# A four-layer convolution chain on one core: the input in three loads, constant products ahead of the first convolution, the result stored pair by pair

## The chip, the cores and the metric

The program runs on one core of a Trainium2 chip. The metric is device time in microseconds (us) of one execution; lower is better. Before the change three executions took 524.96, 528.49 and 530.88 us, so the median is 528.49 us. The engines are TensorE (PE for its matmuls, PEld for its weight loads), VectorE (DVE), ScalarE (ACT), GpSimd (POOL) and SyncE (SP), which only issues transfers. The program has no collective and nothing from another core.

## The reference, cut to what matters

`x` is a tensor of 16 images, 64 channels, 16 by 16 places, float32. Four layers are added to it one after the other, each on a group-normalized copy:

```python
def _gn(v, G=32, eps=1e-05):          # no gamma or beta
    ...
    return ((g - m) / jnp.sqrt(s + eps)).reshape(v.shape)

x = x + _L0_conv_ref(_gn(x), ...)     # 1x1 conv, group norm (8 groups), silu, a gated mixture of Gaussians, 1x1 conv, group norm, silu
x = x + _L1_conv_ref(_gn(x), ...)     # 3x3 depthwise conv and linear attention
x = x + _L2_conv_ref(_gn(x), ...)     # 8-head softmax attention over 256 places
x = x + _L3_conv_ref(_gn(x), ...)     # deformable 3x3 convolution
return x
```

The change touches the first steps of layer 0 and the way in which the result leaves the chip. The first steps of layer 0 are: statistics of `x` by image and pair of channels, `_gn(x)`, the 1x1 convolution with `pre_w`, and the group norm of its result, which has gamma and beta.

## The kernel before, in words

**Layout.** Two images make a pair: the 64 channels of the even image stand on partitions 0 to 63, those of the odd image on 64 to 127, and the 256 places along the free axis. So `x` is one tile of 128 x 8 x 256 floats (1 MB), with 8 pairs (`NP = 8`), and it stays on the chip from the first load to the last store. Each of the four layers is a block of the program in which every engine has its own straight list of instructions. Engines wait for each other by semaphores that count up; at the end of a block all engines meet.

**The head (`layer0`, L243 to L286).** SP (L261 to L267) issues the load of `avg2`, a constant 128 x 128 matrix, then `x` in two halves of four pairs, then all the weights of all four layers, one transfer each, in the order of the layers (`weights.load`, L204). DVE takes the statistics of the eight pairs in order (`bn_stats`, L274); ahead of pair 0 it waits for the first half of `x` and ahead of pair 4 for the second. Then comes `gn_x.vector` (L129): eight aggregations (L140), after which PE multiplies the means by `avg2` (L167), DVE forms the spread of the means (L146 to L148), PE multiplies the variances by `avg2` (L169), DVE adds eps (L150), ACT takes the square root (L174), and DVE makes `scale` (L152) and `shift` (L156, L159). DVE then writes `xn = x * scale + shift` pair by pair (L277). PE convolves two pairs at a time as soon as they are there (L366, four matmuls of 512 columns; a float32 matmul shows as two instructions in the profile). DVE takes the statistics of each convolved pair (L137) and `gn_1` runs in the same way, with `avg8` of the weights of layer 0.

**Steps that order this part.** PE's list is: wait for `avg2`; the two small matmuls of `gn_x`; wait for the weights of layer 0 (`weights.wait`, L209, which wants every one of the 11 transfers of that layer); the four matmuls of the convolution; the two of `gn_1`. POOL fills constant stacks for layer 2 with `memset` (L464, L468), and between the third and the fourth it waits until all eight `xn` are there (L250). ACT has nothing to do in the head but the two square roots. `signals.own` is a counter by which DVE waits for its own last instruction (`Steps`, L83); its count after `gn_x` is `signals.own_steps`.

**`keep_clock` (L177)** is a helper that issues `count` products of `avg2` with itself into a part of PSUM that nobody reads. It is used already at the end of layer 0 (20 of them, 40 instructions in the profile) and in layer 1.

**The rest of layer 0** is a loop over the pairs in which ACT makes squares and exponentials (L415, L418), DVE polynomials and products (L337, L342), and PE sums them up (L382).

**The tail (`layer3`, L1109 to L1568).** Layer 3 goes over the pairs 0 to 7 in order, in nine steps (taps) each. In each step PE spreads weights over rows and columns (L1500, L1510), ACT copies the column part (L1404), DVE multiplies (L1335) and PE sums over the taps (L1523). When a pair is done, DVE adds the sum and the bias to `x[:, n]` (L1339) and raises `added`; `added` starts at 2 (L1322), so it is `n + 3` once pair `n` is final. Nothing reads or writes `x[:, n]` after that in this layer. SP loads the interpolation weights (`hats`, L1236) of two pairs at a time; its last piece of work is `next_chunk(3)`, which issues four transfers for pair 6 and four for pair 7, the latter once enough products of pair 5 have been made. After the block of layer 3 there is a last block (L1593 to L1597), in which SP stores all of `x` in one transfer of 1 MB and waits for it.

Of the kernel before, what the change touches and what calls it, by code (L numbers as in the profile page):

```python
# [24 lines left out]
NP = B // 2  # L25
# [190 lines left out]
def layer0(nc, ins, signals, weights, x, avg2, stacks):  # L216
    with Memory(nc, "L0") as m:
# [14 lines left out]
        s1, s2 = y2[0:32, 4, 0:NP], y2[:, 6, 0:NP]  # L232
        par_ps = y2[:, 4, 0:NP * NPAR].rearrange("p (n k) -> p n k", n=NP)

        avg_in, *x_in = m.sems("avg_in x_in0 x_in1")
        (xn_ready, y1_ready, norm1_ready, z_ready, s1_ready, h1_ready, s2_ready, h2_ready, h2_w_ready,
         par_ready, exp_in, exp_out, coef_ready) = m.sems(
            "xn_ready y1_ready norm1_ready z_ready s1_ready h1_ready s2_ready h2_ready h2_w_ready "
            "par_ready exp_in exp_out coef_ready")
        (uu_ready, e_ready, poly_ready, t_ready, t_used, norm2_ready, out_ready, added, odd_added) = m.sems(  # L240
            "uu_ready e_ready poly_ready t_ready t_used norm2_ready out_ready added odd_added")
# [1 line left out]
        with nc.Block() as block:  # L243
            @block.gpsimd
            def _(pool):

                stacks.fill_q(pool, 0)
                stacks.fill_k(pool, 0)
                stacks.fill_q(pool, 1)
                pool.wait_ge(xn_ready, NP)  # L250
                stacks.fill_k(pool, 1)
                stacks.fill_q(pool, 2)
                pool.wait_ge(norm1_ready, 1)
                stacks.fill_k(pool, 2)
                stacks.fill_q(pool, 3)
                stacks.fill_k(pool, 3)
                for p in range(1, NP, 2):
                    pool.wait_ge(out_ready, p + 1)
                    pool.tensor_tensor(x[:, p, :], x[:, p, :], xn[:, p, :], ALU.add).then_inc(odd_added, 1)

            @block.sync  # L261
            def _(sp):
                sp.dma_start(avg2[:], ins["avg2"]).then_inc(avg_in, 16)
                for h in range(2):
                    half = slice(4 * h, 4 * h + 4)
                    sp.dma_start(x[:, half], ins["x"].rearrange("(n e) c h w -> (e c) n (h w)", e=2)[:, half]).then_inc(x_in[h], 16)
                weights.load(sp, range(4))  # L267

            @block.vector
            def _(dve):  # L270
                for p in range(NP):
                    if p % 4 == 0:
                        dve.wait_ge(x_in[p // 4], 16)
                    dve.bn_stats(signals.x_bn[:, p, :], x[:, p, :]).then_inc(signals.x_stats, 1)  # L274
                gn_x.vector(dve)
                for p in range(NP):
                    dve.tensor_scalar(xn[:, p, :], x[:, p, :], gn_x.scale[:, p:p + 1], gn_x.shift[:, p:p + 1],  # L277
                                      ALU.mult, ALU.add).then_inc(xn_ready, 1)

# [78 lines left out]

            @block.tensor
            def _(pe):  # L360
                pe.wait_ge(avg_in, 16)
                gn_x.tensor(pe)
                weights.wait(pe, 0)
                for h in range(NP // 2):
                    pe.wait_ge(xn_ready, 2 * h + 2)
                    pe.matmul(y1[:, 2 * h:2 * h + 2, :], w_pre[:], xn[:, 2 * h:2 * h + 2, :], start=True, stop=True).then_inc(y1_ready, 1)  # L366
                gn_1.tensor(pe)
                pe.wait_ge(z_ready, NP)
                pe.matmul(s1, w_s1[:], pooled[:], start=True, stop=True).then_inc(s1_ready, 1)
                pe.wait_ge(h1_ready, 1)  # L370
                pe.matmul(s2, w_s2[0:32, :], h1[:], start=True, stop=True).then_inc(s2_ready, 1)
                pe.wait_ge(h2_w_ready, 1)
                pe.matmul(par_ps, same_group[:], h2_w[:], start=True, stop=True).then_inc(par_ready, 1)
                pe.sem_inc(t_used, 2)
                pe.wait_ge(coef_ready, 1)
                with pe.Fori(0, NP // 2) as i:
                    for q in range(2):
                        k = 2 * i + q
                        pe.matmul(y2[:, ds(k, 1), :], w_post[:], z[:, ds(k, 1), :], start=True, stop=False)
                        pe.wait_ge(t_ready, k + 3)  # L380
                        for j in range(NB):
                            mm = pe.matmul(y2[:, ds(k, 1), :], w_post[:], t[:, q, j:j + 1, :], start=False, stop=(j == NB - 1))  # L382
                        mm.then_inc(t_used, 1)
                gn_2.tensor(pe)
                keep_clock(pe, avg2, y1[:, 6], 20)

            @block.scalar
            def _(act):
                gn_x.scalar(act)
                gn_1.scalar(act)  # L390
                act.wait_ge(norm1_ready, 1)
                for p in range(NP):
# [716 lines left out]
                        context(c, 0, k - 6)  # L1109


def layer3(nc, ins, signals, weights, x, avg2):

# [8 lines left out]
    with Memory(nc, "L3") as m:  # L1124
# [97 lines left out]
        with nc.Block() as block:  # L1222
            @block.sync
            def _(sp):
# [43 lines left out]
                sp.wait_ge(later_stored, 256)  # L1268
                for c in range(1, B // CH):
                    next_chunk(c)  # L1270

            @block.gpsimd
            def _(pool):
# [303 lines left out]
def program(nc, ins, out, layers=4):  # L1577
    Memory.semaphores = ExitStack()
    with Memory.semaphores, Memory(nc, "all") as m:
# [9 lines left out]
            if layers > 2:  # L1589
                layer2(nc, ins, signals, weights, x, avg2, stacks)  # L1590
        if layers > 3:
            layer3(nc, ins, signals, weights, x, avg2)
        with nc.Block() as block:  # L1593
            @block.sync
            def _(sp):
                sp.dma_start(out.rearrange("(n e) c h w -> (e c) n (h w)", e=2), x[:]).then_inc(x_out, 16)
                sp.wait_ge(x_out, 16)  # L1597

# [98 lines left out]
```

## Time and profile before

| | |
|---|---|
| three executions | 524.96, 528.49, 530.88 us; median 528.49 us |
| span of the profiled execution | 528.0 us, first to last instruction |
| what lies around the span | not shown apart; the median of the executions is 0.49 us above this span |
| PE, DVE, ACT, POOL busy | 439.1, 342.4, 288.9, 132.8 us |
| layer 0, layer 1, layer 2, layer 3 begin at | 0, 88, 193 and 348 us of the span |

The span runs from the first instruction to the last on any engine. A busy share is an average over stages of different kinds: PE has 83%, but in the first thirteenth of the execution it waits for most of the time. All times in the rows below are microseconds from the start of the span unless they are marked ns. PEclk is the clock that TensorE was granted, as a share of 2.4 GHz.

### The profile page before, as it was taken

To read this page: it belongs to the slowest core of one execution; us is meant where nothing else is said; L and a number is where in the kernel's file an instruction comes from. 1 tells how busy PE (TensorE), PEld (TensorE's weight loads), DVE (VectorE), ACT (ScalarE), POOL (GpSimd) and SP (SyncE) were. 2 spreads that over 40 slices of the span, in tenths; PEclk is the share of its full clock that TensorE was granted. 3 is DMA by queue.
4 is the path that set the end of the run, shared out by engine and by line. 5 is a ranking of instruction groups with operands and counts; after the bars stand their busy time and mean duration, and the time that the engine had idled before them with its cause. 6 is when DMAs were issued, how large, how long until landed. Compare 5 with 4: busy or idle time off the path is not lost. (4 is left out here: it accounts for less than half of the span.)

```text
span 528.0 us, 9368 instructions
## 1 busy us (share of the span) xinstructions
PE 439.1 (83%) x3406; PEld 231.3 (44%) x3406; DVE 342.4 (65%) x668; ACT 288.9 (55%) x511; POOL 132.8 (25%) x162
## 2 busy tenths in 40 slices
PE   0527768899999887679999999939898999999995
PEld 0216648555455664223333333324443454454442
DVE  4549876233344568978999996251654778777784
ACT  1279955131532437047878778722865578486441
POOL 4420004000000005744422212031364428065000
PEclk9956997999999988559999999957977999999999
DMA  5500000900000004952200000016390480933302
GB/s 142 164 0 1 0 0 1 197 1 1 0 1 0 1 0 107 279 175 67 73 27 3 3 2 4 0 47 160 100 226 15 89 181 2 217 55 68 67 2 79
DMA packets 20767, 33.79 MB, mean 64 GB/s; under 512 B 5657, under 2 KB 15497, under 8 KB 19957
## 3 DMA queue, kind: packets, MB, share of 16 engines
q1 hardware_dynamic: 16724, 23.70, 18.9%
q0 software_dynamic: 2176, 6.35, 4.3%
q10 hardware_dynamic: 1824, 3.19, 2.3%
q8 instruction: 26, 0.43, 0.4%
q14 instruction: 17, 0.13, 0.1%
HBM read 16.21 MB, written 4.64 MB: 39 GB/s over the span
## 5 line engine op out<-in xcount | busy, mean ns | idle before, releaser
L1335 DVE TENSOR_TENSOR L_s<-L_row_ps,L_cols 128x1024 f32<-128x1024 f32 x72 | 87.6, 1218 | 9.3 <-PE L_row_ps L1500 7.5
L910 DVE TENSOR_REDUCE L_mx<-L_ring 128x2 f32<-128x512 f32 x128 | 83.3, 686 | 12.4 <-PE L_ring L1034 11.8
L965 ACT ACTIVATE L_e<-L_ring 128x512 f32<-128x512 f32 x128 | 73.7, 597 | 21.4 <-PE L_ring L1047 19.3
L1523 PE MATMUL L_acc<-L_s,L_t_sb 128*64 128x256 f32 x576 | 81.6, 406 | 1.1 <-DVE L_s L1335 1.0
L1404 ACT ACTIVATE L_cols<-L_col_ps 128x512 f32<-128x512 f32 x72 | 42.8, 596 | 48.9 <-PE L_col_ps L1510 48.5
L1034 PE MATMUL L_ring<-stacks_k_st,stacks_q_st 64*128 64x256 bf16 x256 | 51.0, 301 | 7.0 <-DMA stacks_k_st<-L_k_parts 4.7
L1523 PEld LDWEIGHTS L_acc<-L_s,L_t_sb 128*64 128x64 f32 x576 | 36.0, 140 | 35.9 <-DVE L_s L1335 19.8
L1047 PE MATMUL L_ring<-stacks_q_st,stacks_k_st 64*128 64x256 bf16 x256 | 47.2, 282 | 1.2 <-DMA stacks_q_st<-L_m_parts 1.2
L1500 PE MATMUL L_row_ps<-L_hats,L_sel 48*128 48x512 bf16 x144 | 44.6, 392 | 0.0
L1067 PE MATMUL L_ctx_ps<-L_e,L_v_x 128*32 128x256 f32 x512 | 41.5, 398 | 0.0
L1311 DVE COPY L_t_sb<-L_acc 128x192 f32<-128x192 f32 x48 | 17.1, 357 | 31.4 <-PE L_acc L1491 31.4
L1034 PEld LDWEIGHTS L_ring<-stacks_k_st,stacks_q_st 64*128 64x128 bf16 x256 | 15.9, 98 | 43.8 <-DVE L_mx L910 24.2
L382 PE MATMUL L_y<-L_t,all_w_post 128*128 128x256 f32 x96 | 25.3, 418 | 11.5 <-DVE L_t L342 11.5
L1510 PE MATMUL L_col_ps<-L_hats,L_sel 48*128 48x512 bf16 x72 | 28.7, 400 | 7.0 <-DMA L_hats<-L_parts 5.0
L1491 PE MATMUL L_acc<-all_w_all,L_xn 64*128 64x192 f32 x96 | 26.8, 362 | 5.0 <-DVE L_t_sb L1311 2.7
L382 PEld LDWEIGHTS L_y<-L_t,all_w_post 128*128 128x128 f32 x96 | 19.4, 208 | 17.1 <-DVE L_t L342 14.2
L1491 PE MATMUL L_col_ps<-all_w_all,L_xn 64*128 64x192 f32 x96 | 26.7, 360 | 0.0
L853 POOL MEMSET L_v_x<- 128x1024 f32 x1 | 1.0, 951 | 101.7 <-POOLq L496 101.7
L1200 POOL TENSOR_TENSOR L_hat<-L_hat,L_mask 64x768 f32<-64x768 f32 x9 | 16.3, 1812 | 40.1 <-ACT L_hat L1382 40.1
L415 ACT ACTIVATE L_uu<-L_z,L_minus_mu,L_inv 128x256 f32 x48 | 24.4, 586 | 1.3 <-DVEq L314 1.3
L633 ACT ACTIVATE L_sq<-L_t_ps 128x1024 f32<-128x1024 f32 x4 | 4.1, 1024 | 34.9 <-PE L_t_ps L716 34.9
L656 PE MATMUL L_xs_ps<-L_stack,L_w_tap 128*128 128x512 f32 x48 | 22.7, 601 | 0.0
(270 smaller groups left out, 814.2 us busy)
## 6 DMA issues: line engine op xcount, KB each, us to landing
L_hats<-L_parts SPq DMA_DIRECT2D x28, 216.0 KB, 5.0
L_hat<-L_offsets SPq DMA_DIRECT2D x20, 192.0 KB, 4.7
L_mask<-L_offsets SPq DMA_DIRECT2D x10, 192.0 KB, 4.9
stacks_q_st<-L_q_parts SPq DMA_DIRECT2D x12, 128.0 KB, 3.9
stacks_k_st<-L_k_parts ACTq DMA_DIRECT2D x12, 128.0 KB, 4.8
stacks_q_st<-L_q_parts POOLq DMA_DIRECT2D x12, 128.0 KB, 2.7
stacks_k_st<-L_k_parts POOLq DMA_DIRECT2D x12, 128.0 KB, 2.9
L_stack<-L_xpad SPq DMA_DIRECT2D x7, 162.0 KB, 5.8
```

Of the source, the lines that this page charges most:

```text
L382: mm = pe.matmul(y2[:, ds(k, 1), :], w_post[:], t[:, q, j:j + 1, :], start=False, stop=(j == NB - 1))
L910: dve.tensor_reduce(mx[:, n % 2, :, head], ring[:, place(step) % 3].rearrange("p (q s) -> p q s", q=2), AX.X, ALU.max).then_inc(max_read, 1)
L965: act.activation(e[:, k], ring[:, 3 + v % 3], ACT.Exp, scale=HD2 ** -0.5).then_inc(e_ready, 1)
L1034: mm = pe.matmul(ring[:, place(step) % 3, q * N:(q + 1) * N], rows_of(q_st, n, h, p)[:, q * P:(q + 1) * P], rows_of(k_st, n, h, p), start= ...
L1047: mm = pe.matmul(ring[:, 3 + v % 3, t * N:(t + 1) * N], rows_of(k_st, c, h, p)[:, t * P:(t + 1) * P], rows_of(q_st, c, h, p), start=True, ...
L1067: mm = pe.matmul(ctx_ps[32 * j:32 * j + 32, g * N:(g + 1) * N], v_x[:, c % 2, t, 4 * g + j, :], e[:, 4 * g + j, t * N:(t + 1) * N], start= ...
L1335: dve.tensor_tensor(s[:, q], row_ps[:, q], cols[:, t % 3:t % 3 + 1].broadcast_to([P, 2, 2 * N]), ALU.mult).then_inc(s_ready, 1)
L1404: act.activation(cols[:, v % 3], col_ps[:, c % 2], ACT.Copy).then_inc(col_read, 1)
L1491: mm = pe.matmul(out, xn[rows, b, k // 3 * P:(k // 3 + 1) * P], w_all[rows, k % 3 * TW:(k % 3 + 1) * TW], start=True, stop=True)
L1500: mm = pe.matmul(row_ps[:, v % 2, h], sel[0:3 * H, h], hats[0:3 * H, n % 2, :, t * N:(t + 1) * N], start=True, stop=True)
L1510: pe.matmul(col_ps[:, c % 2], sel[C:C + 3 * H, 2], hats[C:C + 3 * H, n % 2, :, t * N:(t + 1) * N], start=True, stop=True).then_inc(col_rea ...
L1523: mm = pe.matmul(acc[C * e:C * e + C, b, 0:N], t_sb[:, b, h, (KK * e + t) * C:(KK * e + t + 1) * C], s[:, q, h, e * N:(e + 1) * N], start= ...
```

## The change

The change has four parts, and one that follows from the second.

1. `x` is loaded in three lots: pairs 0 and 1, pairs 2 and 3, pairs 4 to 7. The load of `avg2` is issued between the first lot and the second. The first lot and `avg2` raise one semaphore (`x_in[0]`), the second and the third lot raise the other (`x_in[1]`). DVE waits for the first two transfers ahead of pair 0 and for both others ahead of pair 2.
2. PE waits for the first lot and `avg2`, issues 20 constant products, then the matmuls of `gn_x`, and after the wait for the weights 8 more constant products ahead of the convolution.
3. ACT writes `xn` for pairs 2, 3, 6 and 7, after waiting for `scale` and `shift`; DVE writes pairs 0, 1, 4 and 5. PE's waits ahead of its four matmuls and POOL's wait ahead of its fourth fill follow that.
4. The last block's store of 1 MB is gone. In layer 3 SP stores each pair (128 KB) when `added` says that it is final, after its last `next_chunk`; the last block only waits for all eight.

```diff
@@ layer0
-        avg_in, *x_in = m.sems("avg_in x_in0 x_in1")
-        (xn_ready, y1_ready, norm1_ready, ...
+        x_in = m.sems("x_in0 x_in1")
+        (xn_ready, xn_by_scalar, y1_ready, norm1_ready, ...
@@ gpsimd
-                pool.wait_ge(xn_ready, NP)
+                pool.wait_ge(xn_ready, 4)
@@ sync
-                sp.dma_start(avg2[:], ins["avg2"]).then_inc(avg_in, 16)
-                for h in range(2):
-                    half = slice(4 * h, 4 * h + 4)
-                    sp.dma_start(x[:, half], ins["x"].rearrange("(n e) c h w -> (e c) n (h w)", e=2)[:, half]).then_inc(x_in[h], 16)
+                for h, lot in enumerate((slice(0, 2), slice(2, 4), slice(4, NP))):
+                    sp.dma_start(x[:, lot], ins["x"].rearrange("(n e) c h w -> (e c) n (h w)", e=2)[:, lot]).then_inc(x_in[min(h, 1)], 16)
+                    if h == 0:
+                        sp.dma_start(avg2[:], ins["avg2"]).then_inc(x_in[h], 16)
                 weights.load(sp, range(4))
@@ vector
                 for p in range(NP):
-                    if p % 4 == 0:
-                        dve.wait_ge(x_in[p // 4], 16)
+                    if p in (0, 2):
+                        dve.wait_ge(x_in[p // 2], 32)
                     dve.bn_stats(signals.x_bn[:, p, :], x[:, p, :]).then_inc(signals.x_stats, 1)
                 gn_x.vector(dve)
-                for p in range(NP):
+                gn_x.scaled = signals.own_steps
+                for p in (0, 1, 4, 5):
                     dve.tensor_scalar(xn[:, p, :], x[:, p, :], gn_x.scale[:, p:p + 1], gn_x.shift[:, p:p + 1],
                                       ALU.mult, ALU.add).then_inc(xn_ready, 1)
@@ tensor
-                pe.wait_ge(avg_in, 16)
+                pe.wait_ge(x_in[0], 32)
+                keep_clock(pe, avg2, y2[:, 6], 20)
                 gn_x.tensor(pe)
                 weights.wait(pe, 0)
+                keep_clock(pe, avg2, y2[:, 6], 8)
                 for h in range(NP // 2):
-                    pe.wait_ge(xn_ready, 2 * h + 2)
+                    pe.wait_ge((xn_ready, xn_by_scalar)[h % 2], 2 * (h // 2) + 2)
                     pe.matmul(y1[:, 2 * h:2 * h + 2, :], w_pre[:], xn[:, 2 * h:2 * h + 2, :], start=True, stop=True).then_inc(y1_ready, 1)
@@ scalar
                 gn_x.scalar(act)
+                act.wait_ge(signals.own, gn_x.scaled)
+                for p in (2, 3, 6, 7):
+                    act.activation(xn[:, p, :], x[:, p, :], ACT.Identity, scale=gn_x.scale[:, p:p + 1],
+                                   bias=gn_x.shift[:, p:p + 1]).then_inc(xn_by_scalar, 1)
                 gn_1.scalar(act)
@@ layer3, sync
                 for c in range(1, B // CH):
                     next_chunk(c)
+                for n in range(NP):
+                    sp.wait_ge(added, n + 3)
+                    sp.dma_start(out.rearrange("(n e) c h w -> (e c) n (h w)", e=2)[:, n], x[:, n]).then_inc(x_out, 16)
@@ program, last block
-                sp.dma_start(out.rearrange("(n e) c h w -> (e c) n (h w)", e=2), x[:]).then_inc(x_out, 16)
-                sp.wait_ge(x_out, 16)
+                sp.wait_ge(x_out, 16 * NP)
```

## Rows read from the trace of the kernel before

**Rows 1.** The page: PE's clock in 40 slices of 13.2 us, in tenths.

```profile
PEclk9956997999999988559999999957977999999999
```

**Rows 2.** Timeline of the head: start, length, engine, line, operation, count, [idle before, releaser].

```profile
0.74 0.40 SPq L263 DMA_DIRECT2D all_avg<-in_avg  x1
1.20 0.96 SPq L266 DMA_DIRECT2D all_x<-in_x  x2
...
5.58 2.90 DVE L274 BATCH_NORM_STATS2 all_x_bn<-all_x 128x6 f32<-128x256 f32 x8 [5.58 <-DMA all_x<-in_x]
...
9.37 0.57 PE L167 MATMUL L_y<-L_gn_x_mv,all_avg 128*128 128x8 f32 x2 [9.37 <-DVEq L144]
...
10.59 0.60 PE L169 MATMUL L_y<-L_gn_x_var,all_avg 128*128 128x8 f32 x2 [0.66 <-DVE L_gn_x_var L148]
...
12.30 2.67 DVE L277 TENSOR_SCALAR L_xn<-all_x,L_gn_x_scale,L_gn_x_shift 128x256 f32<-128x256 f32 x8
13.18 5.88 PE L366 MATMUL L_y<-L_xn,all_w_pre 128*128 128x512 f32 x8 [2.00 <-DVE L_xn L277]
```

**Rows 3.** Instructions of tile x, then of tile avg, issued before 3 us: transfers' time to landing.

```profile
DMA to landing us min/median/max: 4.4/4.9/5.4
...
DMA to landing us min/median/max: 1.9/2.9/3.9
```

**Rows 4.** Timeline of the convolution's passes (weight loads) and the statistics behind them.

```profile
15.02 0.33 PEld L366 LDWEIGHTS L_y<-L_xn,all_w_pre 128*128 128x128 f32 x1 [0.52 <-issue]
15.88 0.33 PEld L366 LDWEIGHTS L_y<-L_xn,all_w_pre 128*128 128x128 f32 x1 [0.52 <-issue]
...
17.58 0.22 PEld L366 LDWEIGHTS L_y<-L_xn,all_w_pre 128*128 128x128 f32 x1 [0.52 <-issue]
18.04 0.19 PEld L366 LDWEIGHTS L_y<-L_xn,all_w_pre 128*128 128x128 f32 x1 [0.24 <-issue]
18.24 1.62 DVE L137 BATCH_NORM_STATS2 L_gn_bn<-L_y 128x6 f32<-128x256 f32 x4 [0.51 <-PE L_y L366]
...
20.92 0.39 PE L167 MATMUL L_y<-L_gn_mv,all_avg 128*128 128x8 f32 x2 [1.85 <-DVEq L144]
```

**Rows 5.** Stretches: length, busy time (instructions) of each engine, PEclk, DMA share, GB/s.

```profile
13.00:17.60 4.60, 4.42 (x6) 1.85 (x7) 3.36 (x11) 0.00 (x0) 2.57 (x2) 1.00 0.57 152
24.00:35.00 11.00, 1.90 (x6) 1.18 (x6) 2.28 (x10) 8.53 (x26) 5.29 (x3) 0.52 0.04 13
80.00:82.00 2.00, 2.00 (x10) 2.00 (x11) 1.16 (x6) 1.83 (x3) 0.00 (x0) 0.50 0.00 0
86.00:87.00 1.00, 1.00 (x11) 1.00 (x10) 0.96 (x4) 0.00 (x0) 0.38 (x1) 1.00 0.00 0
```

**Rows 6.** Timeline of PE: the 20 constant products at the end of layer 0.

```profile
79.75 7.64 PE L182 MATMUL L_y<-all_avg 128*128 128x128 f32 x40
```

**Rows 7.** Lines: ACT's pairwise normalization in layer 3; timeline of ACT at layer 2's start.

```profile
L1413 ACT ACTIVATE L_xn<-all_x,L_gn_shift,L_gn_scale x6: 588/590/591, 408.7 to 492.0; 128x256 f32<-128x256 f32 x6
...
195.16 0.21 ACT L174 ACTIVATE L_gn_sd<-L_gn_sp 128x8 f32<-128x8 f32 x1 [1.17 <-DVE L_gn_sp L150]
198.89 0.69 ACT L953 ACTIVATE L_e<-L_ring,all_l_vec 128x512 f32<-128x512 f32 x1 [3.52 <-PE L_ring L1003]
```

**Rows 8.** Timeline of the tail: SP's last transfers, the last add and the store.

```profile
482.16 11.55 SPq L1236 DMA_DIRECT2D L_hats<-L_parts  x8
...
522.36 0.48 DVE L1339 SCALAR_TENSOR_TENSOR all_x<-L_acc,all_l_vec,all_x 128x256 f32<-128x256 f32 x1 [1.19 <-PE L_acc L1523]
523.12 0.43 SPq L1596 DMA_DIRECT2D out_x<-all_x  x1
```

**Rows 9.** Transfers: the store's landing, a stretch of it, and a 128 KB load.

```profile
out_x<-all_x SPq DMA_DIRECT2D x1, 1024.0 KB, 4.5
...
525.00:526.00 1.00, 0.00 (x0) 0.00 (x0) 0.00 (x0) 0.00 (x0) 0.00 (x0) 1.00 1.03 347
...
all_grid<-in_grid SPq DMA_DIRECT2D x1, 128.0 KB, 2.8
```

More of the change, by code:

```diff
@@ L233, in layer0 @@
         par_ps = y2[:, 4, 0:NP * NPAR].rearrange("p (n k) -> p n k", n=NP)
-        avg_in, *x_in = m.sems("avg_in x_in0 x_in1")
-        (xn_ready, y1_ready, norm1_ready, z_ready, s1_ready, h1_ready, s2_ready, h2_ready, h2_w_ready,
+        x_in = m.sems("x_in0 x_in1")
+        (xn_ready, xn_by_scalar, y1_ready, norm1_ready, z_ready, s1_ready, h1_ready, s2_ready, h2_ready, h2_w_ready,
          par_ready, exp_in, exp_out, coef_ready) = m.sems(
-            "xn_ready y1_ready norm1_ready z_ready s1_ready h1_ready s2_ready h2_ready h2_w_ready "
+            "xn_ready xn_by_scalar y1_ready norm1_ready z_ready s1_ready h1_ready s2_ready h2_ready h2_w_ready "
             "par_ready exp_in exp_out coef_ready")
@@ L1109, in _, with layer3 @@
                         context(c, 0, k - 6)
-def layer3(nc, ins, signals, weights, x, avg2):
+def layer3(nc, ins, signals, weights, x, avg2, out, x_out):
     KK = 9
@@ L1591, in program @@
         if layers > 3:
-            layer3(nc, ins, signals, weights, x, avg2)
+            layer3(nc, ins, signals, weights, x, avg2, out, x_out)
         with nc.Block() as block:
```

## The prediction

> **What bounds the kernel now.** I read four views: the page for the whole, the timeline of the first 20 us, the stretches of TensorE's clock, and the timeline of the last 10 us. The change touches only the two ends of the execution, some 20 us at the start and 6 us at the end, so the question is what ends last at each end, and whether a shift of the start is passed on.
>
> The head is one chain. DVE has nothing until 5.58 us, when the first half of `x` lands [rows 2]. Then the eight statistics run without a gap for 2.90 us, so the second half is not waited for; it was issued about 0.47 us after the first and took 5.4 us, landing at 7.1 us [rows 3]. That is just when DVE comes to pair 4. Aggregation, the two small matmuls at 9.37 and 10.59 us and the small steps between them follow, `xn` begins at 12.30, the convolution at 13.18 and ends at 19.06. PE does nothing before 9.37 us but wait.
>
> The convolution is bound by PE's clock. Its passes (two for each float32 matmul) come 0.86 us apart (15.02, 15.88), the last ones 0.46 us apart (17.58, 18.04) [rows 4]. 512 columns in 0.86 us is the 1.2 GHz level, in 0.46 us near the 2.4 GHz one. The clock column reads 1.00 for the same stretch [rows 5], so in the head I go by the spacing of the passes and not by that column. DVE waits 0.51 us before its last four statistics, which end at 19.86 us; everything behind hangs on that. The clock is low again from 24 to 35 us [rows 5], since PE idles between the few small matmuls there, so what is gained in the head is the time of the convolution and nothing of the later stages.
>
> Over the whole, the page's clock line shows other low stretches, in slices 3 and 4, 17 and 18, and 27 to 31 [rows 1]. Where their borders fall can move when the start is shifted. That is noise for this prediction: three executions of the same kernel spread over 5.9 us.
>
> **The change, part by part.** *Three loads.* The third lot raises the same semaphore as the second, and DVE wants both ahead of pair 2. So pairs 2 and 3 wait for the whole of `x`. The bytes ahead of that moment are the same 1 MB plus 64 KB, the last lot is issued at 2.13 instead of 1.67 us (one more issue of 0.46 us, half of the 0.96 us of two) and the first bytes are asked for at the same 0.74 us, so I keep the landing of all of `x` at 7.1 us, with 6.7 and 7.6 as ends. Pairs 0 and 1 are done before. Six statistics remain at 2.90/8 = 0.36 us each: 7.1 + 2.2 = 9.3 us against 8.48 before. The loads alone cost +0.85 us (0.4 to 1.3). The mean matmul could then start at 9.37 + 0.85 = 10.2 us. The weights are issued 0.46 us later; the convolution waited for `xn` and not for them [rows 2], and it will not start sooner by more than a few tenths in any case below, so that is hidden.
>
> *Twenty constant products.* They stand ahead of the mean matmul on PE's queue, so DVE, and behind it ACT and PE itself, wait for them. They start when the first lot and `avg2` have landed. `avg2` is issued at 1.20 us; the two constants of 64 KB issued in the first 3 us took 1.9 us (alone) and 3.9 us (beside `x`) [rows 3], so it lands between 3.1 and 5.1 us; I take 4.1. The first lot, issued at 0.74, needs no more than the 4.4 us that a lot of twice its size took, so 5.1 at the latest. The 20 products are 40 passes. The same 20 took 7.64 us at the end of layer 0 [rows 6], with ten passes in 2.0 us at the low level (0.21 us each) and eleven in 1 us at the high one [rows 5], where the passes are half as long (0.107 us). All low they would take 8.5 us. In the convolution the low level lasted some 4.4 us from its start (13.18 to 17.6): then 20.6 passes are slow and 19.4 fast, 4.4 + 2.1 = 6.5 us. Between the two cases I take 7.1 us. The products then end at 4.1 + 7.1 = 11.2 us, and the mean matmul starts at 11.2 instead of 9.37: +1.85 us, which contains the 0.85 of the loads.
>
> *At the high level* the two small matmuls are shorter: 0.39 us [rows 4] instead of 0.57 and 0.60 [rows 2], together −0.38 us. *The eight products* are 16 fast passes, 1.7 us. From the variance matmul to the convolution there were 2.59 us; less 0.2 for the faster matmul that is 2.4, and the products fit in it behind the matmul's own time (0.39 + 1.7 = 2.1). I cost them at nothing; all low they are 3.4 us and stick out by some 1.6.
>
> The convolution starts at 13.18 + 1.85 − 0.38 = 14.65 us. Its eight passes at 0.43 us (half of 0.86) put the last start at +3.0, its end at +3.6, and the last two statistics (1.62/4 = 0.4 each) at +4.4 us: 19.05 us instead of 19.86. **The head gives −0.8 us**: −2.25 from the convolution, −0.38 from the small matmuls, +1.85 from the wait behind the products. It would be −1.8 if the products were done in time (loads +0.85 alone), −2.25 with the loads at +0.4.
>
> *ACT's four pairs.* An Identity of one pair takes 0.59 us [rows 7]. ACT is idle there; it delivers pairs 2 and 3 some 1.2 us after `shift`, while PE wants them 0.9 (first two pairs by DVE) + 0.85 us after it. Hidden. DVE comes free 1.3 us sooner, for the first statistics behind the convolution, which at the high clock would otherwise wait about 0.6 us; the sum above contains that. A table load is a possible price, since Identity follows a square root: at 195.16 a square root and at 198.89 an Identity run with no load between them [rows 7], so none. POOL's fourth fill starts when DVE's four are done, about as now; nobody waits for it before layer 2.
>
> *The store.* The last add ends at 522.84, the store is issued at 523.12 (the blocks' meeting lies between) and lands 4.5 us later [rows 8, 9], at 527.6; the span ends 0.4 us after. At 347 GB/s the 1 MB takes 3.0 us of those 4.5; an eighth takes 0.4. So the last pair's store lands 1.9 us after its issue, as the 64 KB load did [rows 3]. Issued at 523.0: 524.9, end 525.3. **The tail gives −2.7 us**; a load of 128 KB beside others took 2.8 us [rows 9], with which it would be −1.8. The other seven stores: SP is done with its hats at 493.71 [rows 8]; by then the adds of pairs 0 to 4 are long done and that of pair 5 about now (the last pair's is at 522.4, two pairs later), so some six stores go out in about 3 us, behind the hats of pair 7, which that pair wants when pair 6 is nearly through. Pair 6 leaves during pair 7. SP has nothing else queued. So they are hidden; without that cover they would be 6 x 0.4 us of transfer.
> The Trainium skill (DMA: Bandwidth & Descriptors, Rules for kernel authors) speaks against this part: it wants many small transfers made one, with 1 MiB or more for full bandwidth. Its fit in the section Anatomy of one DMA, measured on transfers issued by GpSimd, about 2.0 us + bytes/436e3, gives 4.4 us for the old store, and the trace's 4.5 agrees; for the last pair it gives 2.3, by which the tail would be −2.3. The rule does not bite as long as the seven others stay off the path.
>
> **Sum.** 528.0 − 0.8 − 2.7 = 524.5 us of span. The median of the runs shown is 0.49 above that execution's span, so 525.0 us, −3.5 us or 0.66%.
>
> **The rivals.** *Clock up early.* If the clock rises about 4.4 us or less after the first product and `avg2` lands near 3.1 us, the products end by 9.6 us, ahead of the statistics. Then head −1.8 to −2.25, total 523.5 to 524.0. For it: the lower case of the row. Against it: 20 passes too many have to fit, and both conditions must hold.
>
> *The warm-up costs more than it gives*, the slow side. Its place is PE's queue ahead of the mean matmul. With 8.5 us of slow passes from 4.1 the matmul starts at 12.6 (+3.25), nothing is saved on the small ones, the eight products take 3.4 us: variance matmul at 13.85, convolution at 13.85 + 0.6 + 3.4 = 17.85, and slow as before 6.7 us to 24.5 against 19.86: head +4.7, total 528.5 + 4.7 − 2.7 = 530.5 us. It decides as soon as the head loses more than the 2.7 of the tail: a fast convolution that starts after 18.1 us, or a slow one after 15.9. Against it: both times that PE was kept busy, the clock rose within 4.4 and some 6.2 us (13.18 to 17.6, 79.75 to 86) [rows 4, 5].
>
> *The shift is not passed on.* The ends give what I say, but low-clock stretches of the later layers grow or shrink with the shift. The layers' start-ups are chains of short steps on PE, so a border can cost or give 2 us either way; with the spread of the runs 522 to 528.5.
>
> *The change does not do what it says* in one point already: three loads do not let DVE go on with pair 2 earlier. That is in the sum.
>
> **How the numbers follow.** Forecast (524 to 526.5) 0.50; early clock 0.20; products too long 0.08; shifted borders 0.22. A difference of over 1% (5.3 us) is about what a measurement of this kernel can tell from no change. The forecast alone lies 1.8 us short of it: I give 0.08 of its 0.50 to faster, 0.09 of the early clock's, 0.07 of the last, 0.24 in all. Slower needs 533.8 us, which even the slow rival reaches only with a high draw: 0.03. The rest, 0.73, is within 1%. The range: 523.5 less a low draw of 1.7 is 521.8; above, the forecast with the tail at −1.8 and products of 8.5 us is 527.3, and the shifted borders take it to 528.3.
>
> **What would show it.** DVE's statistics end near 9.3 us with a gap of about 2 us behind pair 1 (right), or run on (wrong). PE's first product starts near 4.1 us; the mean matmul starts right behind the last one, later than 10.2. The convolution's passes are 0.43 us apart and its eight take 3.6 us. No table load stands between ACT's square root and its four Identities. The last store lands 1.9 us after its issue, and the span ends some 2.5 us after the last add instead of 5.2. I am wrong if the statistics are not the six behind one wait, if the clock falls again ahead of the convolution, or if the time between 20 us and the last add changes by more than 2 us.

## The result, and the profile after

The changed kernel takes 521.12 us (median of four runs, 520.05 to 522.25) against 527.53 us of the kernel before: ratio 0.988, 95% interval 0.9835 to 0.9925. Six more runs gave 521.48 against 526.94 us, ratio 0.9891 (0.9863 to 0.9919). It is faster by 5.5 to 6.4 us; I had forecast 3.5 us, the right way but too little, and the first median lies 0.7 us under my range. One run of the experiments, 531.19 us, fell into a slower state of the chip and is left out below.

The profiled execution has a span of 519.2 us and took 520.96 us, so 1.8 us lie around a span. That puts the profiled execution of before (span 528.0) at about 529.8 us, a long draw, and not near the median as I had read it.

The head of the changed kernel; columns as in [rows 2]:

```profile
0.74 0.45 SPq L264 DMA_DIRECT2D all_x<-in_x  x1
1.25 0.45 SPq L266 DMA_DIRECT2D all_avg<-in_avg  x1
...
3.81 0.75 DVE L274 BATCH_NORM_STATS2 all_x_bn<-all_x 128x6 f32<-128x256 f32 x2 [3.81 <-DMA all_avg<-in_avg]
...
3.83 6.67 PE L182 MATMUL L_y<-all_avg 128*128 128x128 f32 x40 [3.83 <-DMA all_avg<-in_avg]
...
7.37 2.06 DVE L274 BATCH_NORM_STATS2 all_x_bn<-all_x 128x6 f32<-128x256 f32 x6 [2.81 <-DMA all_x<-in_x]
...
9.46 0.64 DVE L140 BATCH_NORM_AGGREGATE L_gn_x_mv<-all_x_bn 128x2 f32<-128x6 f32 x8
...
10.34 0.29 PE L167 MATMUL L_y<-L_gn_x_mv,all_avg 128*128 128x8 f32 x2
...
11.52 2.03 PE L182 MATMUL L_y<-all_avg 128*128 128x128 f32 x16
...
12.79 2.08 ACT L395 ACTIVATE L_xn<-all_x,L_gn_x_shift,L_gn_x_scale 128x256 f32<-128x256 f32 x4 [0.67 <-DVE L_gn_x_shift L159]
...
13.57 3.70 PE L369 MATMUL L_y<-L_xn,all_w_pre 128*128 128x512 f32 x8
...
18.11 0.64 DVE L140 BATCH_NORM_AGGREGATE L_gn_mv<-L_gn_bn 128x2 f32<-128x6 f32 x8
```

Three things are to be seen. DVE does two statistics and then waits 2.81 us: the second and third load share a semaphore, so pair 2 waits for all of `x`. The products end at 10.50 us, 0.4 us behind DVE's aggregations (10.10); but the mean matmul starts 0.24 us behind the aggregations, as it did before the change (0.21), so in this profile it does not wait for the products. And the convolution takes 3.70 us instead of 5.88 [rows 2], with its passes 0.43 us apart where [rows 4] had 0.86 and 0.46. `gn_1` begins its aggregations at 18.11; in the profile before that was 19.90.

The tail, in the timeline of the changed kernel and in its list of transfers (KB, us to landing):

```profile
516.55 0.48 DVE L1349 SCALAR_TENSOR_TENSOR all_x<-L_acc,all_l_vec,all_x 128x256 f32<-128x256 f32 x1 [1.19 <-PE L_acc L1533]
517.06 0.33 SPq L1280 DMA_DIRECT2D out_x<-all_x  x1
```

```profile
out_x<-all_x SPq DMA_DIRECT2D x1, 128.0 KB, 1.7
```

From the start of the last add to the end of the span it is 2.65 us, against 5.64 before (528.0 − 522.36 [rows 8]): 3.0 us less.

So between these two profiles the ends account for 1.8 + 3.0 = 4.8 us. The head's part varies: over the four profiles with the old head and the five with the changed one in the table below, its means are 19.5 and 18.4 us, which is 1.2 us, and 4.2 for both ends. The two profiles differ by 8.8 us; the other 4 us lie in layers 2 and 3. This table follows milestones through all profiles (us; the last column is the span, the others are the stretches between them). "Old" ends are those of the kernel before, "new" those of the changed one.

| kernel | head, to gn_1's aggregations | to layer 1 | layer 1 | layer 2 | layer 3 to add of pair 0 | pair 0 to last add | last add to end | span |
|---|---|---|---|---|---|---|---|---|
| before | 19.90 | 68.1 | 104.7 | 155.3 | 62.2 | 112.2 | 5.64 | 528.0 |
| before, second profile | 19.74 | 68.1 | 105.2 | 154.8 | 61.1 | 112.1 | 5.63 | 526.6 |
| changed | 18.11 | 67.9 | 105.5 | 153.7 | 59.5 | 111.9 | 2.65 | 519.2 |
| changed, second profile | 18.13 | 67.9 | 105.1 | 154.0 | 60.1 | 111.9 | 2.63 | 519.8 |
| new tail alone | 19.70 | 68.3 | 105.7 | 153.6 | 61.3 | 112.2 | 2.58 | 523.3 |
| new head alone | 18.48 | 67.9 | 105.5 | 153.9 | 59.6 | 112.0 | 5.68 | 523.0 |
| changed, no products | 21.80 | 68.1 | 105.1 | 154.9 | 60.1 | 112.2 | 2.60 | 524.7 |
| own semaphore for each lot | 18.86 | 68.1 | 105.2 | 154.4 | 59.6 | 112.0 | 2.61 | 520.7 |
| early products | 17.21 | 67.9 | 105.4 | 155.0 | 61.1 | 112.0 | 2.61 | 521.2 |
| VectorE alone | 18.37 | 68.1 | 105.1 | 154.5 | 60.7 | 112.1 | 2.59 | 521.4 |
| twelve products | 17.91 | 67.9 | 104.7 | 153.7 | 59.8 | 114.6 | 2.65 | 521.2 |
| changed, products in layer 3 | 18.44 | 68.2 | 104.9 | 154.3 | 56.7 | 111.9 | 2.59 | 517.0 |
| the same, second profile | 18.59 | 68.1 | 105.0 | 152.3 | 57.8 | 112.0 | 2.62 | 516.4 |
| both mended | 18.97 | 67.9 | 104.9 | 155.2 | 57.0 | 111.9 | 2.56 | 518.5 |
| old ends, products in layer 3 | 18.83 | 68.1 | 105.2 | 153.0 | 60.0 | 114.4 | 5.61 | 525.1 |

The column "to layer 1" moves by 0.4 us in all: what the head gains is passed on whole through the rest of layer 0. For the three kernels with two profiles each, layer 2 differs by 0.3 to 2.0 us between the two and layer 3's start-up by 0.6 to 1.1 us; the difference of 2.7 us in that start-up between the first profiles of before and changed is larger than that.

### The profile page after: what moved, and what is told of

Its sections match the earlier page's. It is cut to its first block and busy times, and to the rows that moved or that the text cites. A ratio compares the mean times of both kernels' runs of the same rounds, so it can differ in the third digit from the quotient of the medians.

```text
span 519.2 us, 9486 instructions
## 1 busy us (share of the span) xinstructions
PE 439.2 (85%) x3462; PEld 235.8 (45%) x3462; DVE 341.0 (66%) x664; ACT 291.8 (56%) x515; POOL 133.0 (26%) x162
## 5 line engine op out<-in xcount | busy, mean ns | idle before, releaser
L1533 PE MATMUL L_acc<-L_s,L_t_sb 128*64 128x256 f32 x576 | 79.5, 398 | 1.4 <-DVE L_s L1345 1.2
L1501 PEld LDWEIGHTS L_acc<-all_w_all,L_xn 64*128 64x128 f32 x96 | 18.5, 203 | 9.2 <-DVE L_t_sb L1321 4.3
```

Of the source, the lines that this page charges most:

```text
L1501: mm = pe.matmul(out, xn[rows, b, k // 3 * P:(k // 3 + 1) * P], w_all[rows, k % 3 * TW:(k % 3 + 1) * TW], start=True, stop=True)
L1533: mm = pe.matmul(acc[C * e:C * e + C, b, 0:N], t_sb[:, b, h, (KK * e + t) * C:(KK * e + t + 1) * C], s[:, q, h, e * N:(e + 1) * N], start= ...
```

## The experiments

**The two ends alone.** Theory A: the ends explain the gain, the rest is chance. Theory B: the new head makes later layers faster. Theory C: the pairwise stores help layer 3.

```diff
 # new tail alone: the kernel before, with
+                for n in range(NP):
+                    sp.wait_ge(added, n + 3)
+                    sp.dma_start(out...[:, n], x[:, n]).then_inc(x_out, 16)
 # new head alone: the changed kernel, with the last block's
+                sp.dma_start(out..., x[:]).then_inc(x_out, 16)
```

> The kernel before with nothing but the pairwise store. Theory A (the two ends explain the gain, the rest of the profiled pair's difference is where TensorE's low-clock stretches happened to fall in layer 3): the span ends 2.65 us after the last add instead of 5.64, so 3.0 us less than before, ratio 0.994. Theory B (the head's new timing moves the low-clock stretches of the later layers, every time): also 3.0 us less here, since the head is the old one. Theory C (the stores or the missing 1 MB transfer help layer 3 itself): more than 4.5 us less, and pairs 6 and 7 of layer 3 take less time.

> The changed kernel with the old store of 1 MB in the last block: the changed head alone. Theory A: 1.8 us less than before, ratio 0.9966. Theory B: 3.4 to 5.8 us less, and layer 3 again starts its pair 0 sooner after its own start than before. Theory C: 1.8 us less at most.

The tail alone: 524.53 against 527.43 us, ratio 0.9938 (0.9905 to 0.997), 3.3 us. The head alone: 525.46, ratio 0.9957 (0.9934 to 0.9981), 2.3 us. Both hold what the traces give (3.0 and 1.2 to 1.8); their sum is 5.6 us. Theory C falls: pair 0 to the last add is 112.2 us with the new tail and with the old one. B had wanted 3.4 to 5.8 us of the head alone and stands at the edge of the head's interval of 1.0 to 3.5 us; a smaller effect of the head is not excluded.

**Without the constant products.**

```diff
-                keep_clock(pe, avg2, y2[:, 6], 20)
...
-                keep_clock(pe, avg2, y2[:, 6], 8)
```

> The changed kernel without the 20 and the 8 constant products. Theory A: the passes of the first convolution are 0.86 us apart again for most of it, and the small matmuls take 0.57 us: the head is 0.4 to 0.9 us longer than in the kernel before (statistics 1.0 us later, ScalarE's share little), total 3.0 - 0.6 = 2.4 us less than before, ratio 0.9955. Theory B: as A if it is the clock in the head that carries over, so the same number here.

525.26 us, ratio 0.9961 (0.9934 to 0.9989): 3.7 us more than the changed kernel's 0.9891. The timeline of this kernel's head:

```profile
7.52 2.06 DVE L274 BATCH_NORM_STATS2 all_x_bn<-all_x 128x6 f32<-128x256 f32 x6 [3.05 <-DMA all_x<-in_x]
...
10.46 0.56 PE L167 MATMUL L_y<-L_gn_x_mv,all_avg 128*128 128x8 f32 x2 [10.46 <-DVEq L144]
...
14.28 6.68 PE L367 MATMUL L_y<-L_xn,all_w_pre 128*128 128x512 f32 x8 [2.00 <-DVE L_xn L278]
```

The mean matmul starts at 10.46 us although no product stands ahead of it, and at 10.34 with them. So the loads, not the products, set that time in these two profiles. It is close: in three other profiles with the same head the products took 7.07 to 7.13 us and the mean matmul came at 10.66 to 10.81, some 0.3 to 0.5 us later than the aggregations would have let it. The products give 3.7 us here: 3.0 of the convolution (6.68 to 3.70), 0.4 of the small matmuls. Without them the three loads and ScalarE's share make the head 1.9 us *longer* than before (21.80 against 19.90); I had expected 0.4 to 0.9.

**A semaphore for each lot.**

```diff
+        x_in = m.sems("x_in0 x_in1 x_in2")
...
-                    if p in (0, 2):
-                        dve.wait_ge(x_in[p // 2], 32)
+                    if p in (0, 2, 4):
+                        dve.wait_ge(x_in[p // 2], 16 if p else 32)
```

> The changed kernel with a semaphore of its own for the third load, so that the statistics of pairs 2 and 3 wait for the second lot only. The gap of 2.8 us behind pair 1 shrinks and the statistics end 0.5 to 0.7 us sooner. If the 20 products set the time of the mean matmul (they end at 10.5, the statistics and aggregations at 10.1), the total moves by less than 0.2 us against the changed kernel; if the statistics set it, it falls by 0.6.

520.25 us, ratio 0.9865 (0.9828 to 0.9902), not told apart from the changed kernel. Its head:

```profile
3.69 7.55 PE L182 MATMUL L_y<-all_avg 128*128 128x128 f32 x40 [3.69 <-DMA all_avg<-in_avg]
5.54 0.75 DVE L274 BATCH_NORM_STATS2 all_x_bn<-all_x 128x6 f32<-128x256 f32 x2 [1.11 <-DMA all_x<-in_x]
7.10 1.41 DVE L274 BATCH_NORM_STATS2 all_x_bn<-all_x 128x6 f32<-128x256 f32 x4 [0.81 <-DMA all_x<-in_x]
8.54 0.64 DVE L140 BATCH_NORM_AGGREGATE L_gn_x_mv<-all_x_bn 128x2 f32<-128x6 f32 x8
...
11.08 0.29 PE L167 MATMUL L_y<-L_gn_x_mv,all_avg 128*128 128x8 f32 x2
```

Here the order is clear: the aggregations end at 9.2 us and the mean matmul waits for the products until 11.08. The same 20 products took between 6.16 and 7.55 us in seven profiles, as the clock rose sooner or later. No gain from the earlier statistics is shown, as expected where the products are the bound.

**Early products, and fewer of them.**

```diff
 # early: a semaphore for each load as above; GpSimd fills a tile first, PE works on it before anything has landed
+                pool.memset(warm[:], 1.0).then_inc(coef_ready, 1)
...
+                pe.wait_ge(coef_ready, 1)
+                keep_clock(pe, warm, y2[:, 6], 22)
                 pe.wait_ge(x_in[0], 32)
-                keep_clock(pe, avg2, y2[:, 6], 20)
 # fewer: own semaphores, and
-                keep_clock(pe, avg2, y2[:, 6], 20)
+                keep_clock(pe, avg2, y2[:, 6], 12)
```

> A mended head: a semaphore for each load, and the constant products made of a tile that GpSimd fills first (22 of them), so that they start at about 1.3 us instead of 3.8 and end before the statistics do. The statistics and aggregations end at 9.2 as in the kernel with its own lot, whose mean matmul still waited for the products until 11.1. If the products ahead of the mean matmul are the step that I sized wrongly and the one that still costs, the mean matmul starts at 9.3 to 9.6, gn_1's aggregations at 17.1 to 17.4, and the total falls by 0.8 to 1.6 us against the changed kernel (ratio to before 0.985). If they are hidden by something else, nothing.

> The kernel with a semaphore for each lot, and 12 constant products instead of 20 ahead of the mean matmul. With 20 the mean matmul waited for them until 11.08 us while the aggregations ended at 9.2. All low, 24 passes take 5.1 us: from 3.7 they end at 8.8, so the mean matmul starts at 9.4. If the clock has risen by the time of the convolution, its passes are 0.43 us apart and gn_1's aggregations start at 17.3 us; total 0.8 us under the changed kernel. If 12 are too few to raise it, some passes are 0.86 us apart and the aggregations start at 18 to 19.5 us: no gain or a loss of 1 us.

```profile
0.99 7.71 PE L182 MATMUL L_y<-L_warm 128*128 128x128 f32 x44 [0.99 <-POOL L_warm L247]
...
9.36 0.36 PE L167 MATMUL L_y<-L_gn_x_mv,all_avg 128*128 128x8 f32 x2 [0.66 <-DVEq L144]
...
17.21 0.64 DVE L140 BATCH_NORM_AGGREGATE L_gn_mv<-L_gn_bn 128x2 f32<-128x6 f32 x8
```

These are rows of the early products: the mean matmul starts at 9.36 as before the change, and gn_1 0.9 us sooner than in the changed kernel, as expected. In time it is 520.97 us, ratio 0.9869 (0.9839 to 0.9899) against 0.9891 on the same chip: the right way, not resolved. Twelve products took 5.49 us and were enough to raise the clock (the mean matmul took 0.39 us, the convolution 3.70). But that matmul came at 10.03 and `gn_1` at 17.91, not at 9.4 and 17.3, because all of `x` had landed only at 7.83. Timed they gave 522.01 us and 0.9907 (0.9878 to 0.9937): the expected 0.8 us is not shown.

**ScalarE's share.**

```diff
-                for p in (0, 1, 4, 5):
+                for p in range(NP):
...   # and ACT's four pairs go; the waits of PE and POOL as before the change
```

> The changed kernel with VectorE normalizing all eight pairs again. With the convolution's passes 0.43 us apart, VectorE begins its statistics of the convolved pairs 1.3 us later, of which 0.6 us is not covered: gn_1's aggregations start at 18.7 instead of 18.1 us. The rival: ScalarE's share is hidden and gives nothing, 18.1 as now.

522.2 us, ratio 0.989 (0.9862 to 0.9919) against 0.9891: no difference. By the profile the head is 18.37 instead of 18.11 (18.7 was expected), but DVE goes on behind the mean matmul 0.22 us later as well (10.88 against 10.66), since the last lot landed at 7.61; what is left for the share is 0.04 us. The rival holds: VectorE starts the statistics 0.8 us later, but runs them without a gap, at 0.34 us each.

**Where the rest lies.** The kernel before and the changed one again:

> The kernel before, unchanged, for a second profile. Measured in the first profile: 62.2 us from layer 3's start (ScalarE's table load) to the add of its pair 0, against 59.5 to 59.6 us in the three profiles of kernels with the constant products in the head, and 61.3 and 60.1 in two without. Theory A (the place of the low-clock stretches in layer 3 is a draw of the execution): this time differs from 62.2 and may lie anywhere from 59.5 to 62. Theory B (the head decides it): again 61.5 to 62.5.

> The changed kernel again, for a ratio over more runs and a second profile. The two ends give 4.8 us by the traces, the two halves timed alone 3.3 and 2.3 us, together 5.6. Theory A: ratio 0.989 to 0.991, since the 6.4 us of four runs held a share of chance. Theory B (the parts together do more than each): 0.987 or less.

Layer 3's start-up took 61.1 us where the first profile of before had 62.2, and 60.1 where the changed kernel had 59.5. So it varies by some 1 us from one execution to the next. 61.1 is in A's range and 0.4 us under B's, but it is still above both times of the changed kernel. The changed kernel's ratio of 0.9891 is within A's 0.989 to 0.991. The draws do not mix well: 61.1 to 62.2 in the three profiles with the old head (without products in layer 3), 59.5 to 61.1 in the eight with the new one.

The traces show where the difference arises. Some 34 us into layer 3 PE waits for the first hats. The kernel before, then the changed one (timeline of PE, then stretches as in [rows 5]):

```profile
384.92 1.97 PE L1523 MATMUL L_acc<-L_s,L_t_sb 128*64 128x256 f32 x8 [0.71 <-DVE L_s L1335]
```

```profile
381.00:387.00 6.00, 3.75 (x17) 1.38 (x18) 3.31 (x3) 3.68 (x7) 4.55 (x8) 0.66 0.69 192
387.00:389.00 2.00, 2.00 (x9) 0.77 (x8) 1.11 (x1) 1.07 (x2) 0.12 (x1) 0.50 1.05 268
399.00:405.00 6.00, 4.84 (x22) 2.48 (x24) 1.49 (x2) 4.17 (x8) 3.44 (x2) 0.58 0.01 3
```

```profile
379.53 0.37 PE L1520 MATMUL L_col_ps<-L_hats,L_sel 48*128 48x512 bf16 x1 [1.70 <-DMA L_hats<-L_parts]
381.91 1.08 PE L1533 MATMUL L_acc<-L_s,L_t_sb 128*64 128x256 f32 x8 [0.93 <-DVE L_s L1345]
```

```profile
378.00:384.00 6.00, 3.52 (x24) 1.42 (x26) 3.75 (x4) 4.25 (x8) 4.47 (x8) 1.00 0.79 205
390.00:396.00 6.00, 4.85 (x22) 2.67 (x24) 1.55 (x3) 2.19 (x5) 0.73 (x2) 0.52 0.49 87
```

Before, the clock is low behind this wait (the same eight matmuls take 1.97 us instead of 1.08) and again at 399; in the changed kernel only once, at 390. In all three old-head profiles the wait is 1.94 to 2.08 us and the clock falls behind it. With a new head the wait is 1.70 to 1.86 us; in five of the eight profiles (both of the changed kernel, the new head alone, own semaphores, twelve products) the clock stays up there and the start-up takes 59.5 to 60.1 us, in the other three it falls and the start-up takes 60.1 to 61.1. So the difference is, in the main, one low stretch more or less. Why the hats come later with the old head no run shows, and the wait does not decide alone: of three profiles with 1.70 us the clock fell in one.

In layer 3 PE stands still at the start (348 to 350 us), and its clock is low until the offset convolution has run for some microseconds. Products there test what this costs:

```diff
                 weights.wait(pe, 3)
+                keep_clock(pe, avg2, row_ps[:, 0, 0], 5)
...
                     weigh(0, k, k, k)
+                    if k == 0:
+                        keep_clock(pe, avg2, row_ps[:, 0, 0], 4)
...
+                keep_clock(pe, avg2, row_ps[:, 0, 0], 8)
                 pe.wait_ge(hats_in[0], 64)
```

> The changed kernel with 17 more constant products in layer 3: 5 behind its group norm, 4 behind its first weighing matmuls, 8 ahead of the wait for the first hats. It tests whether low-clock stretches in layer 3's start-up carry the part of the time that neither end explains. From layer 3's start to the add of pair 0 it was 59.5 to 62.2 us in ten profiles. If the stretches matter (theory A), the stretch at the start ends sooner, the four weighings (0.68 us) and the first offset convolution (4.15 us against 2.8) get shorter, and that time falls to 57 to 58.5 us, the total by 1.5 to 2.5 us against the changed kernel. The rival: the chain there is bound by DMA (offsets and hats), the time stays at 59.5 to 61 and the total is unchanged.

> The head with early products and a semaphore for each lot, and the 17 products in layer 3. If both gains hold and add, 0.9 us (head) and 1.5 to 2.5 us (layer 3) under the changed kernel: about 518.5 us, ratio to before 0.983 to 0.985. By the rival of the run before, only the head's 0.9: 520.5.

The changed kernel, then the one with the products (the timeline of PE, then the stretch from 354 to 356 us, columns as in [rows 5]):

```profile
352.89 0.68 PE L1501 MATMUL L_acc<-all_w_all,L_xn 64*128 64x192 f32 x1 [1.84 <-DVE L_t_sb L1321]
...
356.74 4.15 PE L1473 MATMUL L_row_ps<-L_stack,all_w_off 128*32 128x256 f32 x48
```

```profile
354.00:356.00 2.00, 1.21 (x6) 0.71 (x8) 0.65 (x2) 0.63 (x2) 2.00 (x4) 0.50 0.94 199
```

```profile
351.66 1.99 PE L182 MATMUL L_row_ps<-all_avg 128*128 128x128 f32 x8
353.58 0.43 PE L1502 MATMUL L_acc<-all_w_all,L_xn 64*128 64x192 f32 x1
...
356.19 2.80 PE L1474 MATMUL L_row_ps<-L_stack,all_w_off 128*32 128x256 f32 x48
```

```profile
354.00:356.00 2.00, 1.11 (x12) 0.60 (x8) 0.71 (x2) 0.66 (x2) 2.00 (x4) 1.00 1.09 217
```

The clock rises before the weighings instead of during the convolution, which takes 2.80 us instead of 4.15; layer 3's start to the add of pair 0 falls to 56.7 us, in a second profile to 57.8. Timed: 518.9 us, ratio 0.9846 (0.9805 to 0.9887); again, later, 519.63 and 0.9872 (0.984 to 0.9904). With the mended head as well: 520.12 and 0.9847 (0.9806 to 0.9888), where I had expected 518.5 us. So in the profiles the low-clock stretches of this start-up cost 1.7 to 3.4 us; all 17 products came in one edit, and what each place gives is not separated. These kernels have the lowest medians measured, 1.4 to 2.6 us under the changed one, in ratios whose intervals overlap its own.

The mended head did not add its 0.9 us. In that profile the 22 early products were over sooner and `x` came later, and its rows show what follows:

```profile
0.99 6.68 PE L182 MATMUL L_y<-L_warm 128*128 128x128 f32 x44 [0.99 <-POOL L_warm L247]
9.78 0.36 PE L167 MATMUL L_y<-L_gn_x_mv,all_avg 128*128 128x8 f32 x2 [2.11 <-DVEq L144]
11.09 3.12 PE L182 MATMUL L_y<-all_avg 128*128 128x128 f32 x13
```

PE stood still for 2.11 us ahead of the mean matmul (0.66 in the first profile with early products), and the passes of the eight products, of which the last line shows 13, were 0.24 us apart; the granted clock was 0.50 from 12 to 14 us. They took 3.6 us in place of 2.03 and held the convolution up until 14.54; `gn_1` began at 18.97 instead of 17.21.

**Chance or the head?** The same products with the old ends:

> The kernel before with the 17 constant products in layer 3 and nothing else: old head, old store. With the changed ends and these products it was 518.9 us. By the traces the two ends are worth 1.8 + 3.0 = 4.8 us. Theory A (the ends give 4.8 us and the rest of the difference between the two kernels, 1.0 to 1.6 us, is where low-clock stretches of layer 3's start-up fall by chance): 518.9 + 4.8 = 523.7 us, ratio to before 0.994, and layer 3's start to the add of pair 0 takes 56.5 to 57 us as in the two kernels that have the products. Theory B (the changed head makes the later layers faster by 1 us or more): 524.7 us or more, ratio 0.996 or more.

> The changed kernel with the 17 products in layer 3 once more, on the same chip as the one with the old ends. Theory A: 4.3 to 5.3 us under it. Theory B: 6 us or more under it.

525.32 us (520.92 to 528.41, ratio 0.9949, 0.9917 to 0.9982) against 519.63. The difference is 5.7 us by the medians and 0.0077 or 4.1 us by the ratios: A had wanted 4.3 to 5.3, B 6 or more. Layer 3's start-up took 60.0 us; A's 56.5 to 57 did not come, and that is 2.2 to 3.3 us more than in the three profiles with the new head and the same products. It holds two later waits, 1.93 us for hats and 1.95 for ScalarE, where those three have one of 2.75 to 3.02 for hats. The profile shows another reason why the times do not decide:

```profile
414.00:419.00 5.00, 3.55 (x26) 1.89 (x28) 2.44 (x5) 1.55 (x4) 0.00 (x0) 0.98 0.99 229
419.00:422.50 3.50, 3.50 (x17) 1.14 (x13) 2.26 (x2) 1.17 (x3) 0.00 (x0) 0.54 1.03 241
422.50:427.00 4.50, 4.50 (x35) 2.11 (x35) 3.06 (x5) 3.33 (x6) 0.72 (x1) 1.00 1.07 215
```

Here the clock was low for some 3.5 us in the middle of layer 3, right after a wait of 1.45 us for hats at 416 to 418, and the pairs 1 to 7 took 114.4 us instead of 112. The kernel with twelve products has the same at 450 us, behind a wait of 1.36 us. Such a stretch costs 2.4 us and came in 2 of the 15 profiles.

## Why the prediction was wrong

*The head* (forecast −0.8, measured −1.8 against the profile that I had). The step that failed is "the products then end at 11.2 us, and the mean matmul starts at 11.2": the term of +1.85 measured +0.97. Both factors were a little high, the start at 4.1 (3.83; `avg2` landed 2.5 us after its issue) and the length of 7.1 (6.67). The other part of the same step held, and worse than said: the loads alone cost 1.1 us (10.46 against 9.37), not 0.85, because the last lot landed at 7.37 to 7.52 and not at 7.1. So the wait of the mean matmul is mostly the loads', and the products cost 0 to 0.5 us in the changed kernel. From the mean matmul to gn_1 I forecast −2.63 us and it was −2.76. The statement that DVE would wait behind pair 1 for all of `x` is shown by the gap of 2.81 us. The eight products fitted in, as costed.

The profile that I had was itself a draw: its first half of `x` landed at 5.58 us, in the three other profiles with the old head at 4.79 to 5.02, and their mean matmuls started at 8.58 to 8.80. Against the mean of the four, 8.88 us, the five profiles with the changed head (10.25 to 10.81, mean 10.55) are 1.67 us later. Against these the +1.85 was nearly right; the rest of the head gave −2.9, and the whole −1.2. So the head was too small by 0.4 to 1.0 us.

I costed ScalarE's share as hidden in itself but let it cover 0.6 us of VectorE's statistics; it is worth 0.04. I took 0.4 us for a statistic there, and VectorE makes eight in 2.75 us when nothing holds it up.

*The tail* (forecast −2.7, measured −3.0). The mechanism was right. The last store of 128 KB landed after 1.7 us and not 1.9. The seven other stores cost nothing that the traces show: from the add of pair 0 to the last one it is 111.9 to 112.2 us with either store, but for the two profiles with a low-clock stretch in it. The rule of the Trainium skill (DMA: Bandwidth & Descriptors, Rules for kernel authors) against many small transfers did not bite here. By an estimate from its fit for transfers issued by GpSimd (the same page, Anatomy of one DMA) the last store was to take 2.3 us, and the measured 1.7 decides.

*The sum* failed in "528.0 − 0.8 − 2.7": it holds nothing for the time between the ends, which I had put down as noise. What the runs showed in its place is about 1.4 us less in layer 3's start-up (on average 61.5 us in the three old-head profiles, 60.0 in the eight new-head ones), in the form of one low-clock stretch that mostly does not come; layers 1 and 2 differ between the heads by 0.3 us or less on average. Together with 1.2 of the head and 3.0 of the tail that is 5.6 us, and 5.5 to 6.4 were measured. That the place is layer 3's start-up is shown; that the new head causes it is likely and not shown. No mechanism by which the head would reach layer 3 was found, the intervals of the timed runs would also allow chance, and with the head 3.7 us longer and no products in it that stretch took 60.1 us as well. This stays open. The rival of the shifted borders named the place, the start-ups of later layers, and gave it 2 us either way, which is about what they do; the range should have reached lower for it.

"The median of the runs shown is 0.49 above that execution's span" took the profiled execution for a median one; by the 1.8 us around a span it took about 529.8 us. And the three runs shown had a median of 528.49 us, where all later sets have 526.9 to 527.5: of the 3.9 us between my 525.0 and the measured 521.12, 1.0 is this.

Of the rivals, the early clock came nearest (523.5 to 524.0): the products were done in time or nearly so, though `avg2` landed at 3.8 us and not near 3.1. The warm-up that costs more than it gives did not come: all 20 products at the low level would have taken 8.5 us, and none of the seven profiles has more than 7.55.

## What to carry to other kernels

A loading order is worth what its waits let through: three loads behind two semaphores moved the first statistics 1.0 to 1.8 us forward and the end of the last one 0.8 to 1.9 us back. Constant products that fill a wait are free only up to the moment when the real operands are there. Starting them before anything has landed, on a tile that an idle engine fills, took them out of the way in both profiles, but in the one where PE then stood still for 2.11 us the clock was low again behind it, and in the one with 0.66 us it was not. And when the time of one profiled execution is not known, compare its milestones with a second profile before building a sum on it.

## What the runs showed of the hardware

- In the head the clock column does not tell the level. The stretches of the changed kernel, columns as in [rows 5]:

```profile
4.00:6.00 2.00, 2.00 (x10) 2.00 (x11) 0.56 (x2) 0.00 (x0) 2.00 (x2) 1.00 0.96 321
6.00:8.00 2.00, 2.00 (x12) 2.00 (x12) 0.63 (x2) 0.00 (x0) 0.02 (x1) 1.00 0.70 163
8.00:10.00 2.00, 2.00 (x20) 2.00 (x19) 1.97 (x13) 0.00 (x0) 0.00 (x0) 1.00 0.47 107
```

  It reads 1.00 in all three, while PE makes 10, 12 and 20 passes of the same product in 2 us: 0.2 us each, the 1.2 GHz level, and then 0.1, the 2.4 GHz one.
- The clock can fall for some 3.5 us inside a busy stretch, behind a wait of 1.4 to 1.5 us, in some executions and not in others. 73 runs of the kernel before spread from 523.83 to 531.33 us, and the mean granted clock of a run goes loosely with its time: 0.905 at 530.5 us, 0.916 at 525.8.
- With nothing beside it, the last store of 128 KB landed 1.7 us after its issue, one of 1 MB 4.5 us. The eight stores of the changed kernel took 1.7 to 4.0 us, 2.9 in the median.
- Beside the first loads, the same first lot of `x` and `avg2` landed at 3.6 to 4.1 us in eleven profiles, the whole of `x` at 7.1 to 7.8.
